# Attention and quantised FFN on one core: the FFN rows transposed by a DMA in place of TensorE and ScalarE

## The chip, the core and the metric

One NeuronCore of a Trainium2 chip. The metric is the time of one execution on the device in microseconds, the median of several runs. The engines are TensorE (PE, its weight loads PEld), VectorE (DVE), ScalarE (ACT), GpSimd (POOL) and SyncE (SP, which issues the DMAs).

## What is computed

x and ctx have the shape (128, 64, 128): 8192 tokens of 128 features. The reference, cut to what matters:

```
x = x + attention(layernorm(x), ctx, ctx)        # 16 heads of 64, causal, softmax
x = x + ffn(layernorm(x))

def bitlinear(x, w):                             # rows of x are quantised to 8 bits, w to -1, 0, 1
    scale = 127.0 / clip(max(abs(x), axis=-1), 1e-05)
    return einsum('bsi,oi->bso', round(x * scale) / scale, ternary(w))
ffn(x) = bitlinear(silu(bitlinear(x, w_gate)) * bitlinear(x, w_up), w_down)   # inner width 512
```

The change concerns the input of the last bitlinear: 128 tokens x 512 quantised numbers, held as whole numbers in bf16 (`hid_b`). The matmul with w_down needs them with the 512 features on partitions (`hid_t`, four blocks of 128x128).

## The kernel before

The tokens are cut into 64 pairs (two sequences of 64 tokens, 128 rows each), and 16 groups of four pairs. One slot of every engine's program handles one pair in each stage at once; the stages are staggered. In slot s (numbered from 0):

- pair s: scores (TensorE L425), bias and row maximum (VectorE L738, L741), subtraction (GpSimd L866), exponential (ScalarE L570), row sum (VectorE), scaling (GpSimd L884);
- pair s-1: transposes of the probabilities in two halves (TensorE L453 to ps_a, then ps_b), copies to prob_t on ScalarE, attention output (L494), residual x1 (VectorE L801), second layernorm and quantisation, xq;
- pair s-2: transpose of xq (TensorE L438), copy to xq_t (ScalarE), gate and up matmuls (L466, L467), tanh (ScalarE L606), gated, hid, hid_q (VectorE L754, L768, L785), and hid_b (GpSimd L876, signals hb_ready);
- pair s-3: transposes of hid_b (TensorE L446, into the bank ps_b), copy to hid_t (ScalarE, signals ht_evac), down matmul (TensorE L482, signals down_ready), x2 (VectorE L763).

Between these TensorE computes quarters of the next group's keys (k_quarter, L316 to L318, three matmuls of 512 columns each, copied by ScalarE to kp) and of this pair's values (v_quarter, L396 to L398, copied to vp). The last group has no next group, so its slots (60 to 63) have no key quarters. Slots 64 to 66 drain the stages. Every engine takes its program strictly in order; semaphores are the only synchronisation. The transposes of hid_b stand in slots 3 to 66, that is in 64 slots.

The order on TensorE in a slot is: scores, transpose of xq, transposes of hid_b, first half of the probabilities, gate and up (after xq_t), v_quarter 0, second half, k_quarter 0, down matmul, v and k quarters 1, attention output, v and k quarters 2, k_quarter 3, v_quarter 3. In the first slot of a group v_quarter 0 comes ahead of the transpose of xq. After the last slot of a group four transposes of ctx and four of x follow. On ScalarE the order is: xq_t, hid_t, first half of prob_t, tanh, vp and prob_t in turn, kp, vp, exponential, kp, vp, kp, kp, vp.

SP's queue holds all loads and stores. Per group it issues x and ctx of the group after next, x again for the residual (x_res), and the store of the group before.

Of the kernel before, what the change touches and what calls it, by code (L numbers as in the profile page):

```python
# [32 lines left out]
P = 128  # L33
# [7 lines left out]
def build(nc, x, ctx, mask, wq, wk, wv, wo, bo, w_gate, w_up, w_down, ident, causal, chooser, out):  # L41
# [19 lines left out]
    with ExitStack() as es:  # L61
# [9 lines left out]
        ps_h = ps_b[:, 0:F // 2].bitcast(BF16)  # L71
# [53 lines left out]
        id_bf = sb("id_bf", [P, P], BF16)  # L125
# [40 lines left out]
        pt_ready, attn_ready, xqt_ready, gate_ready, up_ready, ht_ready, down_ready = (sem(n) for n in (  # L166
            "pt_ready", "attn_ready", "xqt_ready", "gate_ready", "up_ready", "ht_ready", "down_ready"))

        ctxt_evac, xnt_evac, k_evac, v_evac, pt_evac, xqt_evac, ht_evac, exp_done, tanh_done = (sem(n) for n in (
            "ctxt_evac", "xnt_evac", "k_evac", "v_evac", "pt_evac", "xqt_evac", "ht_evac", "exp_done", "tanh_done"))  # L170
# [38 lines left out]
        def _(sp):  # L209
# [19 lines left out]
            def group(it, par):  # L229

                g = 2 * it + par
                dyn = lambda v, k: v[g + k] if isinstance(it, int) else v[bass.ds(g + k, 1)].rearrange(
                    "o p q d -> (o p) q d")
                if group_ahead(it, par * GP, 2):
                    sp.wait_ge(xn_ready, GP * g + GP)
                    sp.dma_start(x_in[par][:], dyn(x_g, 2)).then_inc(x_loaded[par], 16)
                    sp.wait_ge(ctxt_ready, g + 1)
                    sp.dma_start(ctx_in[par][:], dyn(ctx_g, 2)).then_inc(ctx_loaded[par], 16)
                if group_ahead(it, par * GP, 1):
                    if not isinstance(it, int) or g:  # L240
                        sp.wait_ge(x1_done, GP * g)
                    sp.dma_start(x_res[1 - par][:], dyn(x_g, 1)).then_inc(xres_loaded[1 - par], 16)
                if not isinstance(it, int) or g:
                    sp.wait_ge(x2_done, GP * g)
                    sp.dma_start(dyn(out_g, -1), x1[1 - par][:]).then_inc(stored[1 - par], 16)

            for it in range(BODIES):
                for par in range(2):
                    group(it, par)
# [10 lines left out]
        def _(pe):  # L260
# [116 lines left out]
            def slot(it, c):  # L377
# [64 lines left out]
                if live(it, c, 3):  # L442

                    pe.wait_ge(hb_ready, s - 2)
                    for k in range(FB):
                        t = nc.tensor.transpose(ps_h[:, k * P:(k + 1) * P], hid_b[:, k * P:(k + 1) * P], id_bf[:])  # L446
# [468 lines left out]
```

## Time and profile before

| | |
|---|---|
| median of 3 runs | 815.12 us (815.04 to 815.55) |
| the profiled execution | 815.8 us, span 814.0 us |
| busy: TensorE, VectorE, ScalarE, GpSimd | 783.2, 677.9, 678.6, 406.9 us |
| granted TensorE clock over the span | 0.993 of full speed |
| DMA packets' share of the 16 DMA engines, SP's queue | 8.5% |
| setup: cast of id_bf on VectorE at 4.99 us | 0.21 us, and then 0.56 us of waiting for a mask matmul (L268) |

The busy time of an engine includes overlap of pipelined instructions, so a busy TensorE is not one at its peak. The idle time of an engine that is not the bottleneck costs nothing. A row of the timeline says when an instruction (or several alike, "x4") starts, for how long it is recorded, and in brackets how long its engine stood idle ahead of it and for whom.

### The profile page before, as it was taken

The page shows a single profiled execution, that of the slowest core. Times are in us where ns is not written, and L with a number is a line of the kernel's source. Part 1 is how long each engine was busy: PE and PEld are TensorE (multiplying, and loading weights), DVE is VectorE, ACT ScalarE, POOL GpSimd, SP SyncE. Part 2 cuts the span into 40 slices and gives each one's busy share as a digit, 9 for nine tenths or more (in the row PEclk, how much of TensorE's full clock was granted, in tenths as well). Part 3 has the DMA queues.
Part 4 walks back from the last instruction along what each step waited for, and adds up shares of the span by engine and source line. Part 5 has one row for each costly group of instructions (what it writes and reads, how often), then busy time and mean ns, then how long its engine had stood idle before and what let it go on. Part 6 is the DMA issues. An engine that isn't in the chain of part 4 may idle for free.

```text
span 814.0 us, 15482 instructions
## 1 busy us (share of the span) xinstructions
PE 783.2 (96%) x5487; PEld 543.7 (67%) x5550; DVE 677.9 (83%) x1845; ACT 678.6 (83%) x1202; POOL 406.9 (50%) x404
## 2 busy tenths in 40 slices
PE   7899999999999999999999999999999999999983
PEld 5657667666766766666676676676676667667652
DVE  7749888888888888888888888888888888878894
ACT  4688888888888888988888888888888888888872
POOL 1234545455455555555555545555455554544551
PEclk9999999999999999999999999999999999999997
DMA  7200010000101001010100101010010100000000
GB/s 219 61 1 1 15 39 16 22 18 14 41 13 40 5 17 33 14 41 14 39 1 14 41 14 40 14 40 2 13 41 14 40 14 15 0 14 14 2 14 14
DMA packets 37123, 20.84 MB, mean 26 GB/s; under 512 B 1460, under 2 KB 36534, under 8 KB 37046
## 3 DMA queue, kind: packets, MB, share of 16 engines
q1 hardware_dynamic: 37046, 19.84, 8.5%
q8 instruction: 45, 0.74, 0.4%
q14 instruction: 32, 0.26, 0.1%
HBM read 15.64 MB, written 4.19 MB: 24 GB/s over the span
## 4 chain that ended last, share of the span: by engine, by line
PE 91%; DVE 4%; ACT 2%; issue 2%; POOL 1%; DMA 0%; POOLq 0%; DVEq 0%
PE ps_s L425 14%; PE ps_a L494 14%; PE ps_s L396 5%; PE ps_s L316 4%; PE ps_kv L396 4%; PE ps_kv L397 3%; PE ps_kv L316 3%; PE ps_kv L317 3%; PE ps_s L318 3%; PE ps_s L398 3%; PE ps_s L397 3%; PE ps_b L453 3%; PE ps_s L317 3%; PE ps_kv L398 3%; PE ps_kv L318 3%; PE ps_a L453 3%
## 5 line engine op out<-in xcount | busy, mean ns | idle before, releaser
L866 POOL TENSOR_TENSOR prob<-prob,row_max 128x1024 f32<-128x1024 f32 x64 | 121.9, 1905 | 179.6 <-DVE row_max L741 179.6
L514 ACT ACTIVATE vp<-ps_s 64x512 f32<-64x512 f32 x256 | 151.2, 591 | 33.2 <-PE ps_s L398 28.9
L884 POOL TENSOR_TENSOR prob<-prob,row_rec 128x512 f32<-128x512 f32 x128 | 130.7, 1042 | 56.5 <-DVE row_rec L816 56.5
L514 ACT ACTIVATE vp<-ps_kv 64x512 f32<-64x512 f32 x256 | 151.5, 592 | 5.3
L876 POOL TENSOR_TENSOR hid_b<-hid_q,neg_round 128x512 bf16<-128x512 f32 x64 | 66.5, 1039 | 124.3 <-DVE hid_q L785 124.3
L494 PE MATMUL ps_a<-vp,prob_t 128*64 128x128 f32 x2048 | 125.9, 276 | 1.3 <-DVE x L763 1.2
L494 PEld LDWEIGHTS ps_a<-vp,prob_t 128*64 128x64 f32 x2048 | 110.6, 137 | 24.3 <-issue 16.3
L425 PE MATMUL ps_s<-kp,xn_t 128*64 128x512 f32 x512 | 124.0, 605 | 2.9 <-ACT vp L514 1.9
L738 DVE TENSOR_TENSOR prob<-ps_s,bias_sb 128x1024 f32<-128x1024 f32 x64 | 78.4, 1225 | 51.8 <-PE ps_s L425 51.7
L843 POOL TENSOR_TENSOR rs<-ve,neg_half 128x1 f32<-128x1 f32 x128 | 70.2, 548 | 42.0 <-DVE ve L663 25.0
L514 ACT ACTIVATE kp<-ps_s 128x512 f32<-128x512 f32 x130 | 77.8, 598 | 11.8 <-PE ps_s L284 8.0
L741 DVE TENSOR_REDUCE row_max<-prob 128x16 f32<-128x1024 f32 x64 | 78.1, 1220 | 2.2
L814 DVE TENSOR_REDUCE row_sum<-prob 128x16 f32<-128x1024 f32 x64 | 77.4, 1210 | 0.0
L514 ACT ACTIVATE kp<-ps_kv 128x512 f32<-128x512 f32 x122 | 72.3, 593 | 0.6 <-PE ps_kv L284 0.5
L425 PEld LDWEIGHTS ps_s<-kp,xn_t 128*64 128x64 f32 x512 | 31.0, 136 | 60.4 <-issue 55.3
L514 ACT ACTIVATE xq_t<-ps_u 128x128 bf16<-128x128 f32 x64 | 17.8, 278 | 62.7 <-PE ps_u L438 62.7
L570 ACT ACTIVATE prob<-prob 128x1024 f32<-128x1024 f32 x64 | 66.9, 1045 | 0.0
L396 PE MATMUL ps_s<-n_hi,ct_hi 128*128 128x512 f32 x128 | 62.5, 489 | 0.7 <-ACT vp L514 0.7
L396 PE MATMUL ps_kv<-n_hi,ct_hi 128*128 128x512 f32 x128 | 61.4, 480 | 0.0
L316 PE MATMUL ps_kv<-ct_hi,m_hi 128*128 128x512 f32 x120 | 52.5, 438 | 1.0 <-ACT wd_t L514 1.0
L754 DVE SCALAR_TENSOR_TENSOR gated<-tanh_sb,ps_g 128x512 f32<-128x512 f32 x64 | 43.9, 687 | 10.2 <-ACT tanh_sb L606 8.8
L316 PE MATMUL ps_s<-ct_hi,m_hi 128*128 128x512 f32 x128 | 52.0, 406 | 0.3
(175 smaller groups left out, 1734.8 us busy)
## 6 DMA issues: line engine op xcount, KB each, us to landing
x_in<-in_x SPq DMA_DIRECT2D x16, 256.0 KB, 3.9
ctx_in<-in_ctx SPq DMA_DIRECT2D x16, 256.0 KB, 4.4
x_res<-in_x SPq DMA_DIRECT2D x16, 256.0 KB, 2.8
out<-x SPq DMA_DIRECT2D x15, 256.0 KB, 2.5
kp<-in_L_xattn_Wk SPq DMA_DIRECT2D x1, 512.0 KB, 3.7
kp<-in_L_xattn_Wq SPq DMA_DIRECT2D x1, 512.0 KB, 4.6
kp<-in_L_xattn_Wv SPq DMA_DIRECT2D x1, 512.0 KB, 5.5
kp<-in_L_xattn_Wo SPq DMA_DIRECT2D x1, 512.0 KB, 6.1
```

The costliest lines, as they stand in the source:

```text
L316: mm(dst, hi, ct_hi[par][:], start=True, stop=False)
L396: mm(v_dst, ct_hi[par][:, cols], hi, start=True, stop=False)
L425: t = mm(ps_s[b * S:(b + 1) * S, half * BANK:(half + 1) * BANK], xn_t[par][:, cols], kp[par][:, half * 8:half * 8 + 8, cols], start=True, ...
L494: t = mm(ps_a[b * S:(b + 1) * S, 0:D], prob_t[:, a, b * S:(b + 1) * S], vp[(c - 1) % 2][:, b, a, :], start=(a == 0), stop=(a == HP - 1))
L514: copy = lambda dst, src, **kw: nc.scalar.activation(dst, src, ACT.Copy, **kw)
L570: nc.scalar.activation(prob[c % 2][:], prob[c % 2][:], ACT.Exp).then_inc(exp_done, 1)
L738: v.tensor_tensor(prob[c % 2][:], ps_s[:, :].rearrange("p (h j) -> p h j", j=S), pair_bias.broadcast_to([P, H, S]), ALU.add).then_inc(bias ...
L741: v.tensor_reduce(row_max[c % 2][:], prob[c % 2][:], AX, ALU.max).then_inc(max_done, 1)
L814: v.tensor_reduce(row_sum[:], prob[c % 2][:], AX, ALU.add).then_inc(sum_step, 1)
L843: p.tensor_tensor(dst[:], src[:], neg_half[:], ALU.pow).then_inc(done, 1)
L866: p.tensor_tensor(prob[c % 2][:], prob[c % 2][:], rows(row_max[c % 2]), ALU.subtract).then_inc(shifted, 1)
L884: p.tensor_tensor(prob[c % 2][:, heads, :], prob[c % 2][:, heads, :], rows(row_rec[c % 2])[:, heads, :], ALU.mult).then_inc(normed, 1)
```

## The change

The four transposes of hid_b on TensorE and the copy to hid_t on ScalarE go away, and with them the bf16 identity id_bf and its cast in the setup. SP issues one transposing DMA from SBUF to SBUF per pair: once hid_b is written and the previous down matmul has read hid_t. The down matmul waits for that DMA (ht_moved), as does GpSimd's next write of hid_b. SP's loads and stores are laid out slot by slot around it: the store of the group before in the last slot of a group ahead of the transpose, x_res in its second slot and x and ctx in its third slot behind the transpose. The waits of loads and stores on the compute engines are the same; x and ctx are now asked for by the group three ahead.

```
@@ SP
-            def group(it, par):
-                ... x_in and ctx_in of group g+2, x_res of group g+1, store of group g-1
+            def load_inputs(g):
+                par = g % 2
+                sp.wait_ge(xn_ready, GP * (g - 2) + GP)
+                sp.dma_start(x_in[par][:], x_g[g]).then_inc(x_loaded[par], 16)
+                sp.wait_ge(ctxt_ready, g - 1)
+                sp.dma_start(ctx_in[par][:], ctx_g[g]).then_inc(ctx_loaded[par], 16)
+            def slot(it, c):
+                s = BODY * it + c
+                g, q, par = 2 * it + c // GP, c % GP, c // GP % 2
+                if q == 3 and g > 0 and live(it, c):
+                    sp.wait_ge(x2_done, GP * g)
+                    sp.dma_start(out_g[g - 1], x1[1 - par][:]).then_inc(stored[1 - par], 16)
+                if live(it, c, 3):
+                    sp.wait_ge(hb_ready, s - 2)
+                    if live(it, c, 4):
+                        sp.wait_ge(down_ready, s - 3)
+                    sp.dma_start_transpose(hid_t[:, :, :], hid_b[:, :]).then_inc(ht_moved, 16)
+                if q == 1 and live(it, c) and group_ahead(it, c, 1):
+                    if g:
                         sp.wait_ge(x1_done, GP * g)
+                    sp.dma_start(x_res[1 - par][:], x_g[g + 1]).then_inc(xres_loaded[1 - par], 16)
+                if q == 2 and live(it, c) and group_ahead(it, c, 3):
+                    load_inputs(g + 3)
+            load_inputs(2)
+            slots(slot, 3)
@@ TensorE
-                if live(it, c, 3):
-                    pe.wait_ge(hb_ready, s - 2)
-                    for k in range(FB):
-                        t = nc.tensor.transpose(ps_h[:, k * P:(k + 1) * P], hid_b[:, k * P:(k + 1) * P], id_bf[:])
-                    t.then_inc(ht_ready, 1)
@@ TensorE, second half of the probabilities
-                    if live(it, c, 3):
-                        pe.wait_ge(ht_evac, s - 2)
@@ TensorE, down matmul
-                    pe.wait_ge(ht_evac, s - 2)
+                    pe.wait_ge(ht_moved, 16 * (s - 2))
@@ ScalarE
-                if live(it, c, 3):
-                    act.wait_ge(ht_ready, s - 2)
-                    copy(flat(hid_t[:, :, :]), ps_h[:, :]).then_inc(ht_evac, 1)
@@ VectorE, setup
-            dve.wait_ge(id_in, 16)
-            v.tensor_copy(id_bf[:], id_sb[:]).then_inc(const_set, 1)
@@ GpSimd, before hid_b
-                        pool.wait_ge(ht_ready, s - 2)
+                        pool.wait_ge(ht_moved, 16 * (s - 2))
```

## Rows read from the trace of the kernel before

**Rows 1.** Busy time of each engine in a stretch: engine busy (count), clock, DMA.

```profile
105.40:405.40 300.00, 298.54 (x2104) 206.46 (x2128) 257.07 (x710) 260.50 (x464) 158.74 (x157) 1.00 0.09 25
...
746.00:795.00 49.00, 43.42 (x344) 29.75 (x346) 43.43 (x117) 40.38 (x72) 28.27 (x26) 1.00 0.02 7
...
795.00:814.00 19.00, 6.38 (x60) 4.26 (x59) 9.50 (x30) 3.57 (x7) 2.62 (x3) 0.69 0.05 15
```

**Rows 2.** The same view for hid_b alone, steady stretch.

```profile
105.40:405.40 300.00, 9.66 (x100) 8.73 (x100) 25.97 (x25) 1.00 0.09 25
```

**Rows 3.** Timeline of a plain slot: start, duration, engine, line, operation, idle before.

```profile
407.38 0.39 PE L446 MATMUL ps_b<-id_bf,hid_b 128*128 128x128 bf16 x4
...
407.58 0.28 ACT L514 ACTIVATE xq_t<-ps_u 128x128 bf16<-128x128 f32 x1 [0.69 <-PE ps_u L438]
...
407.60 0.61 PE L453 MATMUL ps_a<-id_sb,prob 128*128 128x128 f32 x4
...
407.94 0.10 PEld L466 LDWEIGHTS ps_g<-wg_t,xq_t 128*128 128x128 bf16 x1
```

**Rows 4.** Timeline of the same slot: hid_b, down matmul, next hid_b.

```profile
402.38 1.04 POOL L876 TENSOR_TENSOR hid_b<-hid_q,neg_round 128x512 bf16<-128x512 f32 x1 [1.74 <-DVE hid_q L785]
...
410.32 0.40 PE L482 MATMUL ps_a<-wd_t,hid_t 128*128 128x128 bf16 x4
...
414.04 1.04 POOL L876 TENSOR_TENSOR hid_b<-hid_q,neg_round 128x512 bf16<-128x512 f32 x1 [1.74 <-DVE hid_q L785]
```

**Rows 5.** Timeline of slot 65: xq_t and the gate's weight load.

```profile
803.21 0.28 ACT L514 ACTIVATE xq_t<-ps_u 128x128 bf16<-128x128 f32 x1 [6.75 <-PE ps_u L438]
...
803.54 0.10 PEld L466 LDWEIGHTS ps_g<-wg_t,xq_t 128*128 128x128 bf16 x1 [0.21 <-ACT xq_t L514]
```

**Rows 6.** Waits from 100 to 700 us: total, times, longest.

```profile
PEld ps_s L316 <- ACT kp L514: 5.5, 12, 0.5
```

**Rows 7.** Timeline of the first slot of a group, parts.

```profile
420.89 0.61 PE L453 MATMUL ps_a<-id_sb,prob 128*128 128x128 f32 x4
...
421.09 0.60 ACT L514 ACTIVATE hid_t<-ps_b 128x512 bf16<-128x512 bf16 x1
...
421.58 0.59 ACT L514 ACTIVATE prob_t<-ps_a 128x512 f32<-128x512 f32 x1
...
427.01 0.40 PE L397 MATMUL ps_s<-n_lo,ct_hi 128*128 128x512 f32 x1
...
427.24 0.39 PE L398 MATMUL ps_s<-n_hi,ct_lo 128*128 128x512 f32 x1
...
427.66 0.19 PEld L316 LDWEIGHTS ps_s<-ct_hi,m_hi 128*128 128x128 f32 x1 [0.46 <-ACT kp L514]
```

**Rows 8.** Timeline of slot 64, VectorE.

```profile
796.00 0.69 DVE L754 SCALAR_TENSOR_TENSOR gated<-tanh_sb,ps_g 128x512 f32<-128x512 f32 x1 [2.22 <-ACT tanh_sb L606]
```

**Rows 9.** DMA issues: KB each, us from issue to landing.

```profile
ctx_in<-in_ctx SPq DMA_DIRECT2D x16, 256.0 KB, 4.4
...
id_sb<-c_ident SPq DMA_DIRECT2D x1, 64.0 KB, 1.8
```

**Rows 10.** Timeline of the last slots: hid_b, down matmul, its use.

```profile
780.20 1.04 POOL L876 TENSOR_TENSOR hid_b<-hid_q,neg_round 128x512 bf16<-128x512 f32 x1 [1.49 <-DVE hid_q L785]
...
786.32 0.39 PE L482 MATMUL ps_a<-wd_t,hid_t 128*128 128x128 bf16 x4
...
799.56 1.04 POOL L876 TENSOR_TENSOR hid_b<-hid_q,neg_round 128x512 bf16<-128x512 f32 x1 [5.05 <-DVE hid_q L785]
...
804.37 0.63 PE L482 MATMUL ps_a<-wd_t,hid_t 128*128 128x128 bf16 x4
...
805.51 0.34 DVE L763 SCALAR_TENSOR_TENSOR x<-ps_a,o_scale,x 128x128 f32<-128x128 f32 x1
...
808.47 1.04 POOL L876 TENSOR_TENSOR hid_b<-hid_q,neg_round 128x512 bf16<-128x512 f32 x1 [7.31 <-DVE hid_q L785]
...
810.86 0.61 PE L482 MATMUL ps_a<-wd_t,hid_t 128*128 128x128 bf16 x4 [0.69 <-ACT hid_t L514]
```

More of the change, by code:

```diff
@@ L70, in build @@
         ps_b = ps("ps_b", 1)
-        ps_h = ps_b[:, 0:F // 2].bitcast(BF16)
         ps_g = ps("ps_g", 1)
@@ L124, in build @@
         hid_b = sb("hid_b", [P, F], BF16)
-        id_bf = sb("id_bf", [P, P], BF16)
         hid_t = sb("hid_t", [P, FB, P], BF16)
@@ L165, in build @@
             "ctxt_ready", "xnt_ready", "k_ready", "v_ready", "scores_ready"))
[L166 to L170, printed above, removed]
+        pt_ready, attn_ready, xqt_ready, gate_ready, up_ready, ht_moved, down_ready = (sem(n) for n in (
+            "pt_ready", "attn_ready", "xqt_ready", "gate_ready", "up_ready", "ht_moved", "down_ready"))
+        ctxt_evac, xnt_evac, k_evac, v_evac, pt_evac, xqt_evac, exp_done, tanh_done = (sem(n) for n in (
+            "ctxt_evac", "xnt_evac", "k_evac", "v_evac", "pt_evac", "xqt_evac", "exp_done", "tanh_done"))
         ctlo_ready, biased, max_done, sum_step, ln1_step, xn_ready = (sem(n) for n in (
@@ L227, in _ @@
             sp.dma_start(x_res[0][:], x_g[0]).then_inc(xres_loaded[0], 16)
-            def group(it, par):
[L231 to L240, printed above, removed]
-                        sp.wait_ge(x1_done, GP * g)
[L242 to L245, printed above, removed]
@@ L247, in _ @@
-            for it in range(BODIES):
-                for par in range(2):
-                    group(it, par)
+            def load_inputs(g):
[17 more added lines that the diff above has]
+                    if g:
+                        sp.wait_ge(x1_done, GP * g)
+                    sp.dma_start(x_res[1 - par][:], x_g[g + 1]).then_inc(xres_loaded[1 - par], 16)
+                if q == 2 and live(it, c) and group_ahead(it, c, 3):
+                    load_inputs(g + 3)
@@ L334, in _ @@
                     pe.wait_ge(absum_done, 3)
-                    pe.wait_ge(const_set, 4)
+                    pe.wait_ge(const_set, 3)
                     mm(ps_kv[:, 0:3], ones_sb[:], f_sum[:, 0:3], start=True, stop=True).then_inc(mean_ready, 1)
```

## The prediction

> **What bounds the kernel now.** I read the busy time by stretch first. In the steady part TensorE is busy 298.54 of 300 us; in the 49 us of the last group (no next group to prepare) it is busy 43.42 and VectorE 43.43; in the last 19 us TensorE has 6.38 us of work, so the tail is latency [rows 1]. One slot handles one pair, and 25 slots fit in 300 us, 12.0 us each on average [rows 2]. So the question in 58 of the 64 affected slots (3 to 60) is how much earlier TensorE reaches its next instruction, and not how busy ScalarE is.
>
> Next I read the timeline around the removed instructions [rows 3]. In a plain slot (third or fourth pair of a group, some 11.66 us from one hid_b to the next [rows 4]) TensorE transposes xq (released xq_t), then hid_b (407.38), then the first half of the probabilities (407.60), then loads the weights of the gate matmul (407.94). That load needs xq_t, which ScalarE finishes at 407.58 + 0.28 = 407.86. The reader should see that the removed transposes stand between a request and its answer: xq goes out to ScalarE, and TensorE does 0.22 + 0.34 us of other work until the answer is back.
>
> **What is removed from TensorE.** Four transposes of hid_b per slot (100 in 25 slots [rows 2]), which overlap each other; what they add to the queue is the distance from their start to the next instruction's, 407.60 - 407.38 = 0.22 us [rows 3]. Taken off in full that is 58 x 0.22 = 12.8 us. It does not come off in full: without them the probability transposes start at 407.38 and the gate's weight load could start 0.22 earlier, at 407.72, but xq_t is finished only at 407.86. Of the wake-up, the tail has a row in which TensorE really waits: xq_t ends at 803.21 + 0.28 = 803.49, the load starts at 803.54, 0.05 later [rows 5]. So the load moves from 407.94 to 407.91. The gain is 0.03 us per slot, 58 x 0.03 = 1.7 us; the other 0.19 turns from work into waiting for xq_t. ScalarE has been idle for 0.69 us when xq arrives [rows 3], so it can't answer sooner when its hid_t copy is gone.
>
> **What is removed from ScalarE.** One copy of 0.60 us per slot [rows 7]. It pays only where ScalarE makes TensorE wait. That is once per group: in its first slot the load of L316 waits 0.5 us for a kp copy, 12 times in the 600 us [rows 6]. There ScalarE runs from xq_t to that kp copy without a gap. The copy of the first half of the probabilities starts at 421.58, behind hid_t; without it, it starts as soon as its transposes end, 420.89 + 0.61 - 0.22 = 421.28, so about 0.3 earlier, which two queued neighbours leave at 0.27. TensorE's matmuls here follow each other at 0.23 us (L397 at 427.01, L398 at 427.24); L316 starts 0.42 us after L398 (427.24 to 427.66), so 0.19 us is lost to ScalarE, and 0.27 covers it [rows 7]. 14 such slots (4, 8, ... 56) x 0.19 = 2.7 us. In slot 64 VectorE waits 2.22 us for tanh [rows 8], which stands behind the same pair of copies: 0.3 us. In slots 61 to 63 VectorE starts its work back to back; I cost them at nothing, hidden by VectorE's 43.43 us; without that cover it would be 0.03 each.
>
> **What is added: the transpose by DMA.** Call T the time from hid_b's last write to the moment TensorE may load hid_t: SP's wake-up, issue, transfer, completion. No row of before shows such a transfer. From below: 64 KB plain takes 1.8 us from issue to landing; from above among plain ones: 256 KB behind another 256 KB takes 4.4 us [rows 9]. This one moves 128 KB inside the chip; I take the middle of these, T = 3.0. A reordering transfer may be slower than any plain one, so what hides it matters more:
> - Plain slots: hid_b ends at 402.38 + 1.04 = 403.42, the down matmul (L482) starts at 410.32: 6.90 us of cover, and all of T disappears behind TensorE's own matmuls.
> - Slots 61 to 64: 781.24 to 786.32, 5.08 us of cover.
> - Slot 65: 800.60 to 804.37, 3.77 us, and VectorE takes the result (L763) only at 805.51, 0.51 after the matmul ends at 805.00; so it costs from about T = 4.2.
> - Slot 66: nothing covers it. Hid_b ends at 809.51 and the matmul starts at 810.86, 1.35 us for transposes, copy and hand-overs; in place of them stands T. Cost T - 1.35 = 1.65 us.
> All of these are read in [rows 4, 10].
>
> The new wait of SP is on hb_ready and on the previous down matmul, which ends at 410.72 where the next hid_b ends at 415.08, so hb_ready is always last [rows 4]. Behind it in SP's queue stand loads and stores. The x_res load and the loads three groups ahead are issued right behind a transpose, some 8 us before or about where they were issued, and have slots of 12 us to land; the store of a group is issued before that slot's transpose as its x2 is complete earlier. Only in the drain does something queue: the store of three quarters of the last group, ready at about 805.9, now waits until the transpose of slot 66 is issued near 809.6; it hides behind the very last store, which can't be issued before x2 of the last pair, near 812. GpSimd's new wait (transfer before the next hid_b) has a whole slot, 11.66 - T. VectorE loses one small cast in the setup, after which it waited for TensorE (the table of the profile above): nothing.
>
> The page "VectorE: DVE Perf Modes" of the Trainium skill, section "The three transpose paths", speaks against the change: 390 ns on TensorE against 1309 ns by the DMA crossbar for a 128x128 bf16 block, and its rules for authors prefer TensorE where PSUM will do. Here TensorE pays 0.22 us for four blocks in its queue [rows 3], so for TensorE the trace is lower than the page; for the crossbar no row here can tell. Four times 1309 is an estimate of 5.2 us by that page; by it the sum below would come out at about no change.
>
> **Sum, T = 3.0:** -1.7 (TensorE queue) - 2.7 (first slots of groups) - 0.3 (slot 64) + 1.65 (slot 66) = -3.05 us. The profiled execution took 815.8 us with a span of 814.0; the median of the runs is 815.12, and I take the difference to it: 812.1 us.
>
> **Rivals.**
> - Full queue gain. If the wait for xq_t is shorter than I read, all 0.22 us come off in 58 slots: 11.1 us more gain, 801.0. For it: TensorE is the bound at 99.5% in the steady part. Against: 407.86 and 407.94 above [rows 3]. 0.07.
> - Transfer of middle length, T from 4.4 to 5.3: the steady part still hides it, but slot 66 costs 3.1 to 4.0, slot 65 0.2 to 1.1 and slots 61 to 64 up to 1.0 together. Sum from -1.5 to +1.4: no change, 813.6 to 816.5. The sum of the skill's estimate falls here. 0.20.
> - Longer, T from 5.3 to 6.9: the last group pays in four slots. At 6.7: -4.7 + 5.35 + 2.5 + 4 x 1.65 = +9.8, 825. 0.07.
> - The transfer becomes the bound (the slower side): its place is the loop down matmul, x2, hid, hid_q, hid_b, transpose, next down matmul. From L482 at 410.32 to the end of the next hid_b (414.04 + 1.04 = 415.08) are 4.76 us [rows 4, 10], so a slot can't be shorter than 4.76 + T, and against the mean of 12.0 [rows 2] this decides from T of about 7.0 to 7.2. Four blocks one after another, each at the 1.8 us of the 64 KB row [rows 9], would give T = 7.2: then the gains are gone, and the end costs 5.85 + 3.0 + 4 x 2.1 = 17: 832 us. Each further microsecond of T adds some 57 us. For it: a transfer that writes 2-byte elements in another order has no plain row as its equal. Against: 6.9 us is much for 128 KB. 0.14.
>
> **Chances and range.** My forecast (T up to 4.4, small queue gain) 0.52, its own range 810.5 to 814. With the 0.07 of the full gain: faster 0.59. Within 0.2% (1.6 us, about what can be told): the middle length, 0.20. Slower: 0.07 + 0.14 = 0.21. The range 808 to 826 holds the forecast, the middle and the longer case and, below, a queue gain of up to twice what I expect; it leaves out the full gain and the transfer as bound, together 0.21.
>
> **What would show it.** (1) Transposes gone from TensorE, and in their place an idle of about 0.2 us before the gate matmul's weight load, released by xq_t: right. No such idle and slots 0.2 us shorter: full gain. (2) The 0.5 us wait of L316 for kp gone in first slots of groups. (3) Landing of the transpose against the start of L482: over 3 us of room in plain slots; a wait of L482 for DMA there would make me wrong. (4) From the last hid_b to the last L482 about 3.0 us instead of 1.35. (5) The prediction fails most cheaply by T: above 4.4 the gain is gone, above 7 it turns into a large loss.

## The result, and the profile after

| | before | after |
|---|---|---|
| median of 4 runs | 815.34 us (815.04 to 816.84) | 807.38 us (807.29 to 807.77) |
| ratio to before | | 0.990, 95% interval 0.9883 to 0.9915 |
| span of the profiled execution | 814.0 us | 805.3 us |
| busy: TensorE, ScalarE | 783.2, 678.6 us | 776.1, 653.8 us |

The change makes the kernel 8.0 us faster. Later runs beside other kernels gave 806.42 us (806.2 to 806.91) for the same code, ratio 0.9887 (0.9874 to 0.9901). The forecast was faster, by 3.05 us.

From the page of the changed kernel: span, busy time, DMA packets, SP's queue, and the issues of the new transfer (the last number is the median time from issue to landing).

```profile
span 805.3 us, 15033 instructions
...
PE 776.1 (96%) x5294; PEld 527.6 (66%) x5294; DVE 678.5 (84%) x1844; ACT 653.8 (81%) x1138; POOL 407.0 (51%) x404
...
DMA packets 71937, 29.19 MB, mean 36 GB/s; under 512 B 36277, under 2 KB 71351, under 8 KB 71863
...
q1 hardware_dynamic: 71862, 28.24, 13.7%
...
hid_t<-hid_b SPq DMA_TRANSPOSE x64, 2.5
```

The unknown of the prediction, the transfer's time, is in the last line: 2.5 us. SP's queue goes from 8.5% to 13.7% of the DMA engines' time. The busy time says nothing on the gain: TensorE still counts as busy all the time in the steady stretch, which answers to the first row of [rows 1]:

```profile
105.40:405.40 300.00, 300.00 (x2052) 202.79 (x2049) 261.03 (x714) 254.23 (x445) 160.57 (x159) 1.00 0.14 36
```

TensorE's recorded instructions overlap, so a hole of a tenth of a microsecond doesn't show in this sum, and the gain has to be read from distances between starts. I take the start of the gate matmul's weight load (L466 in both kernels) as the mark of a slot.

| stretch | before | after | difference |
|---|---|---|---|
| up to the first mark (slot 2) | 61.20 | 60.26 | -0.94 |
| slot 2 to 3 | 11.26 | 11.22 | -0.04 |
| slots 3 to 59, 56 steps | 670.96 | 661.62 | -9.34 |
| slots 59 to 63 | 41.22 | 40.96 | -0.26 |
| 63 to 64, 64 to 65 | 9.80, 9.10 | 9.82, 9.46 | +0.38 |
| slot 65's mark to the end of the last hid_b | 5.97 | 5.96 | -0.01 |
| end of the last hid_b to the last down matmul | 1.35 | 2.54 | +1.19 |

The sum is -9.02 us; the store behind the last work takes 0.3 us more, and the spans differ by 8.7 us. Inside the 56 steps the median step from a group's first slot to its second goes from 11.32 to 11.05 us (-0.27, 14 times), the other three steps of a group by 0.13 each (11.66 to 11.53, 11.67 to 11.53, 13.29 to 13.16; 42 times): 14 x 0.27 + 42 x 0.13 = 9.2 us. This trace is on the long side: a second trace of the same code (e15) has 11.51 us for the plain slots and 660.78 us for the 56 steps, 10.2 us less than before.

The plain slot of the changed kernel, which answers to [rows 3, 4]: start, duration, engine, line, operation, in brackets the idle time and its releaser.

```profile
401.71 0.33 PE L444 MATMUL ps_u<-id_sb,xq 128*128 128x128 f32 x1
...
401.88 0.60 PE L453 MATMUL ps_a<-id_sb,prob 128*128 128x128 f32 x4
...
402.08 0.28 ACT L512 ACTIVATE xq_t<-ps_u 128x128 bf16<-128x128 f32 x1 [0.69 <-PE ps_u L444]
...
402.41 0.10 PEld L466 LDWEIGHTS ps_g<-wg_t,xq_t 128*128 128x128 bf16 x1 [0.17 <-ACT xq_t L512]
...
402.41 0.39 PE L466 MATMUL ps_g<-wg_t,xq_t 128*128 128x512 bf16 x1
...
402.64 0.38 PE L467 MATMUL ps_u<-wu_t,xq_t 128*128 128x512 bf16 x1
...
404.69 0.40 PE L480 MATMUL ps_a<-wd_t,hid_t 128*128 128x128 bf16 x4
```

The reader is to see two things. The weight load now waits 0.17 us for xq_t, and it and its matmul start at the same time, 402.41. And from the transpose of xq (401.71) to the up matmul (402.64) are 0.93 us. In the kernel before, where that transpose starts at 407.21, it is 1.05 us to 408.26; three rows of its timeline:

```profile
407.21 0.33 PE L438 MATMUL ps_u<-id_sb,xq 128*128 128x128 f32 x1
...
408.05 0.10 PEld L467 LDWEIGHTS ps_u<-wu_t,xq_t 128*128 128x128 bf16 x1
...
408.26 0.38 PE L467 MATMUL ps_u<-wu_t,xq_t 128*128 128x512 bf16 x1
```

The two matmuls follow each other at some 0.22 us, so before the change the gate matmul started at about 408.04 (its own record is missing), 0.10 us after its weights had been loaded at 407.94. The load was ahead of its matmul then; it set nothing.

The waits of the changed kernel from 100 to 700 us (total, times, longest), which answer to [rows 6]:

```profile
PEld ps_g L466 <- ACT xq_t L512: 8.5, 51, 0.2
...
PEld ps_s L322 <- ACT kp L512: 4.8, 12, 0.4
```

The wait for xq_t is in all 51 slots of the stretch, 0.17 us each. The wait for the kp copy in the first slots of groups is still there, 0.1 us shorter.

The end of the kernel, timeline, which answers to the last rows of [rows 10]:

```profile
798.26 1.04 POOL L869 TENSOR_TENSOR hid_b<-hid_q,neg_round 128x512 bf16<-128x512 f32 x1 [7.15 <-DVE hid_q L778]
...
799.33 1.19 SPq L246 DMA_TRANSPOSE hid_t<-hid_b  x1
...
801.84 0.61 PE L480 MATMUL ps_a<-wd_t,hid_t 128*128 128x128 bf16 x4 [7.04 <-DMA hid_t<-hid_b]
```

Nothing covers the transfer here, so T can be read off: from 798.26 + 1.04 = 799.30 to 801.84, 2.54 us: 0.03 until SP issues, 2.45 for the DMA, 0.05 until TensorE starts. The page "VectorE: DVE Perf Modes" of the Trainium skill, section "The three transpose paths", gives 1309 ns for one 128x128 block; four of them would be an estimate of 5.2 us. The trace gives half of that for the four blocks moved by one instruction, and the trace decides.

### The profile page after: what moved, and what is told of

It reads as the page before. It is cut to its first block, busy times and chain, and to the rows that moved or that the text cites. A ratio compares the mean times of both kernels' runs of the same rounds, so it can differ in the third digit from the quotient of the medians.

```text
span 805.3 us, 15033 instructions
## 1 busy us (share of the span) xinstructions
PE 776.1 (96%) x5294; PEld 527.6 (66%) x5294; DVE 678.5 (84%) x1844; ACT 653.8 (81%) x1138; POOL 407.0 (51%) x404
## 2 busy tenths in 40 slices
DMA packets 71937, 29.19 MB, mean 36 GB/s; under 512 B 36277, under 2 KB 71351, under 8 KB 71863
## 3 DMA queue, kind: packets, MB, share of 16 engines
q1 hardware_dynamic: 71862, 28.24, 13.7%
## 4 chain that ended last, share of the span: by engine, by line
PE 89%; DVE 7%; issue 1%; DMA 1%; ACT 1%; POOL 1%; POOLq 0%; DVEq 0%
PE ps_s L431 14%; PE ps_a L492 14%; PE ps_s L402 5%; PE ps_s L322 4%; PE ps_kv L402 4%; PE ps_kv L322 4%; PE ps_s L403 3%; PE ps_s L324 3%; PE ps_s L404 3%; PE ps_kv L323 3%; PE ps_s L323 3%; PE ps_kv L403 3%; PE ps_kv L324 3%; PE ps_kv L404 3%; PE ps_a L453 3%; PE ps_b L453 3%
## 5 line engine op out<-in xcount | busy, mean ns | idle before, releaser
L512 ACT ACTIVATE kp<-ps_s 128x512 f32<-128x512 f32 x130 | 77.7, 598 | 11.9 <-PE ps_s L290 8.1
L322 PE MATMUL ps_kv<-ct_hi,m_hi 128*128 128x512 f32 x120 | 52.6, 438 | 1.0 <-ACT wd_t L512 1.0
L322 PE MATMUL ps_s<-ct_hi,m_hi 128*128 128x512 f32 x128 | 52.0, 406 | 0.0
L403 PE MATMUL ps_s<-n_lo,ct_hi 128*128 128x512 f32 x128 | 50.7, 396 | 0.0
```

The lines of the kernel that those rows point to most:

```text
L322: mm(dst, hi, ct_hi[par][:], start=True, stop=False)
L403: mm(v_dst, ct_hi[par][:, cols], lo, start=False, stop=False)
L512: copy = lambda dst, src, **kw: nc.scalar.activation(dst, src, ACT.Copy, **kw)
```

## The experiments

Each kernel was timed against the kernel before on the same chip; ratios are to it. "Plain slot" is the median of the second and third of a group's four steps, "first slot" the step from the first slot of a group to its second. After: 11.53 (e15: 11.51) and 11.05 us; before: 11.66 and 11.32 us.

### e1: the setup's cast put back

```
+            dve.wait_ge(id_in, 16)
+            v.tensor_copy(id_bf[:], id_sb[:]).then_inc(const_set, 1)
...
-                    pe.wait_ge(const_set, 3)
+                    pe.wait_ge(const_set, 4)
```

> The changed kernel with only the setup's cast of id_bf, its wait for the identity and TensorE's count of four put back; nothing uses id_bf. Theory (the 0.9 us that the setup is shorter comes from the moment at which TensorE's matmuls go from double to single duration, not from the cast): 807.4 us give or take 0.9, and the transposes of the setup change their duration from about 1.06 us for four to 0.60 at one place or the other. Rival (the cast and its wait delayed the setup): 808.3 us, with VectorE's work after the cast later by 0.2 us or more.

Measured: 807.58 us (806.59 to 808.43), ratio 0.9894 (0.9879 to 0.9908). The slots are those of the changed kernel (first slot 11.04, 56 steps 661.34). The first mark is at 61.08, near the 61.20 of before; but the changed kernel run again, without the cast, had it at 61.22. So the cast is not what the 0.94 us of the setup came from. What differs is read from TensorE's timeline in the setup. Before:

```profile
12.11 1.06 PE L274 MATMUL ps_g<-id_sb,ctx_in 128*128 128x128 f32 x4
...
12.96 1.06 PE L284 MATMUL ps_a<-id_sb,kp 128*128 128x128 f32 x4
...
13.81 0.65 PE L284 MATMUL ps_b<-id_sb,kp 128*128 128x128 f32 x4
```

After:

```profile
11.90 0.60 PE L280 MATMUL ps_g<-id_sb,ctx_in 128*128 128x128 f32 x4
...
12.34 0.60 PE L290 MATMUL ps_a<-id_sb,kp 128*128 128x128 f32 x4
...
12.78 0.60 PE L290 MATMUL ps_b<-id_sb,kp 128*128 128x128 f32 x4
```

The same four transposes take 1.06 us in one trace and 0.60 in the other, and the moment of the change differs by over a microsecond. The changed kernel run again (e15) has the 1.06 us of the kernel before at this place. Over the seventeen traces the first mark lies anywhere from 60.26 to 62.35. What moves it was not settled; it belongs to no edit that was tried.

### e2 and e3: four or two transposes of hid_b back on TensorE, with the DMA kept

The results of these transposes are not used; ScalarE copies nothing and hid_t still comes by DMA. GpSimd waits for them before it writes the next hid_b. The bf16 identity and its cast, which e1 tested, come back with them.

```
+                if live(it, c, 3):
+                    pe.wait_ge(hb_ready, s - 2)
+                    for k in range(4):          # e3: range(2)
+                        t = nc.tensor.transpose(ps_h[:, k * P:(k + 1) * P], hid_b[:, k * P:(k + 1) * P], id_bf[:])
+                    t.then_inc(ht_ready, 1)
```

> The changed kernel with the four transposes of hid_b put back on TensorE at their old place, their result unused; hid_t still comes by DMA and ScalarE has no copy. Theory (0.13 us per slot came off TensorE's queue in 58 slots, and 0.14 us more in 14 first slots of groups came from ScalarE): 7.5 us come back, about 814.9 us, slots of 11.66 us and first-slot to second-slot distances of 11.18 us. Rival (the queue term was 0.03 per slot as predicted and ScalarE's copy gave the rest): 809.1 us.

> The same with two of the four transposes put back (0.11 us of queue in place of 0.22). Theory (the gate matmul starts at the later of two moments: the end of the matmuls queued ahead of it, and the arrival of xq_t): two transposes end 0.02 us after xq_t's arrival, so only 0.02 us per slot, 1.2 us in all: 808.6 us. Rival (what is taken off the queue pays in proportion): half of 7.5 us, 811.1 us.

Measured: e2 816.91 us (816.16 to 819.23), ratio 1.0014 (1.0004 to 1.0023); e3 809.99 us (809.37 to 810.19), ratio 0.9924 (0.9908 to 0.9941). Over the 56 steps e2 takes 670.57 us, against 670.96 before and 661.62 after: 8.95 of the 9.34 us come back with the four transposes alone. Plain slots take 11.66 in e2, but 11.54 to 11.56 in e3: the first two transposes cost about 0.02 us (0.03 to 0.05 against e15) and the next two 0.11. So the 0.22 us that four of them occupy is not what is saved; the gate matmul starts at the later of two moments, the end of the queue ahead of it or the arrival of xq_t. First slots take 11.28 in e2 and 11.17 in e3, so there each pair costs about 0.12.

The timeline of e2 has the record that is missing in the kernel before:

```profile
407.75 0.61 PE L462 MATMUL ps_a<-id_sb,prob 128*128 128x128 f32 x4
...
408.09 0.10 PEld L475 LDWEIGHTS ps_g<-wg_t,xq_t 128*128 128x128 bf16 x1
...
408.20 0.38 PE L475 MATMUL ps_g<-wg_t,xq_t 128*128 128x512 bf16 x1
...
408.41 0.38 PE L476 MATMUL ps_u<-wu_t,xq_t 128*128 128x512 bf16 x1
```

With the four transposes in the queue the gate's load (408.09) runs 0.11 us ahead of its matmul (408.20), which starts 0.45 us, four transposes at 0.11, after 407.75. Without them both start together. This is the point at which the prediction went wrong.

### e4: ScalarE's copy back, with the DMA kept

```
+                if live(it, c, 3):
+                    act.wait_ge(hb_ready, s - 2)
+                    copy(hid_x[:], hid_b[:, :]).then_inc(ht_evac, 1)
```

The copy reads hid_b itself and its result is not used; GpSimd waits for it as well.

> The changed kernel with ScalarE's copy of 128x512 bf16 put back at its old place, reading hid_b in SBUF and writing a spare tile (the old one read PSUM); TensorE has no transposes. Theory: the first slots of groups lose what they had gained, 14 x 0.14 us, and the other slots nothing: 809.3 us. Rival (the copy was what held up most slots): 814.9 us.

Measured: 810.71 us (810.62 to 810.89), ratio 0.9933 (0.9918 to 0.9947). Plain slots stay at 11.51, first slots go to 11.30, 0.25 above the changed kernel. The wait for the kp copy grows (waits from 100 to 700 us):

```profile
PEld ps_s L323 <- ACT kp L513: 7.9, 12, 0.7
```

So the copy costs nothing in plain slots and a quarter of a microsecond once per group, 14 x 0.25 = 3.5 us; the time rose by 3.3. With e2, either half of the removed work is enough to lose nearly all of the 0.27 us there: TensorE's 0.22 us alone (e2) or ScalarE's 0.60 us copy alone (e4). A first slot that is as long as the slower of two paths, TensorE's and ScalarE's, and gets shorter only if both do, fits all four lengths: 11.32 with both (before), 11.28, 11.30, and 11.05 with neither.

### e5: more work ahead of the gate matmul

If TensorE idles 0.09 us for xq_t, independent work ahead of the gate matmul should fill it. Here that is the whole v_quarter 0 (three matmuls), and in the first slots the second half of the probabilities.

```
+                if early:
+                    second_half()
+                    gate_up()
+                elif group_ahead(it, c, 1):
+                    v_quarter(0)
+                    gate_up()
+                    second_half()
```

> The changed kernel with other work between the transpose of xq and the gate matmul: v_quarter 0 ahead of gate and up in plain slots, the second half of the probabilities' transposes ahead of them in first slots. Theory (what is left of the removed transposes' 0.22 us, 0.09 us per slot, is waiting for xq_t): 58 x 0.09 = 5.2 us less, 802.2 us, and no wait of the gate's weight load for xq_t. Rival (tanh comes 0.7 us later and VectorE, which has 0.85 us to spare before it needs it, is held up together with what follows): 807 to 810 us.

Measured: 810.04 us (809.13 to 810.86), ratio 0.9931 (0.9916 to 0.9946). Over the 56 steps it takes 662.64 us, against 660.78 and 661.62 in two traces of the changed kernel. The wait for xq_t is gone and the one for the kp copy, which was in first slots only, is now in every slot (waits from 100 to 700 us):

```profile
PEld ps_s L322 <- ACT kp L525: 17.8, 51, 0.7
```

In a plain slot the up matmul now starts 1.54 us after the transpose of xq, 0.61 later than in the changed kernel, and ScalarE's tanh 1.74 us after it, 0.44 later; behind tanh stand the kp copies. TensorE waits 0.25 us for one of them, and the plain slot is 11.49 us, so of the 0.09 about 0.02 is gained. The loss is in the first slots, where the second half of the probabilities was moved. Here the edit shifts the mark itself, so I take VectorE's row maximum instead: from a group's first slot to its second it is 11.97 us, against 11.79 in e15, 14 times. My theory that the order would bring the gain was wrong for this size of move: ScalarE became what TensorE waits for. The rest of the distance to 807.38 lies at the two ends of the kernel, and the section on the prediction shows how much these scatter.

### e6: the last pair by TensorE and ScalarE

```
-                if live(it, c, 3):
+                if live(it, c, 3) and not (s - 3 >= PAIRS - 1):
                     ... dma_start_transpose
+                if live(it, c, 3) and s - 3 >= PAIRS - 1:
+                    ... four transposes on TensorE, and the copy on ScalarE, as before
```

> The changed kernel, but the very last pair's hid_b (slot 66) is transposed by TensorE and copied by ScalarE as before the change. Theory (the drain lost 2.54 - 1.35 = 1.2 us to the transfer): 806.2 us. Rival (the end is set by the stores, so the transfer hides): 807.4 us.

Measured: 804.67 us (804.44 to 805.87), ratio 0.9868 (0.9854 to 0.9883). The end of its timeline:

```profile
798.45 1.04 POOL L891 TENSOR_TENSOR hid_b<-hid_q,neg_round 128x512 bf16<-128x512 f32 x1 [7.30 <-DVE hid_q L797]
...
799.54 0.61 PE L455 MATMUL ps_b<-id_bf,hid_b 128*128 128x128 bf16 x4 [4.56 <-POOL hid_b L891]
...
800.19 0.60 ACT L524 ACTIVATE hid_t<-ps_b 128x512 bf16<-128x512 bf16 x1 [5.33 <-PE ps_b L455]
...
800.84 0.61 PE L492 MATMUL ps_a<-wd_t,hid_t 128*128 128x128 bf16 x4 [0.69 <-ACT hid_t L524]
```

From hid_b's end to the down matmul are 1.35 us again, in place of 2.54. That is the loss of the drain, 1.2 us, taken back where nothing covers the transfer. The whole time fell by more, 2.7 us against the first runs of the changed kernel and 1.75 against e15; the two other pairs with this edit give 1.9 (e10 to e11) and 1.1 (e13 to e14). Of these only the 1.2 is seen at its place.

### e7, e8, e9: one, three and five further transposes ahead of the real one

They go to buffers that nobody reads, and make T longer.

```
+                    for i in range(n):
+                        sp.dma_start_transpose(hid_x[i][:, :, :], hid_b[:, :]).then_inc(extra_moved, 16)
                     sp.dma_start_transpose(hid_t[:, :, :], hid_b[:, :]).then_inc(ht_moved, 16)
```

> The changed kernel with one more transposing DMA of hid_b, into a spare tile, issued ahead of each real one. Theory (a transfer is hidden as long as it lands within the cover): landing comes later by one issue, 1.2 us, to about 3.7 us; the steady part does not change, slot 66 pays 1.2: 808.6 us. Rival (the transfers' traffic itself slows the engines or the loads): 57 slots longer by a visible amount, 812 us or more.

> Three more transposing DMAs ahead of each real one. Theory: landing at about 2.5 + 3 x 1.2 = 6.1 us; the plain slots' cover of about 6.6 us still hides it; slots 61 to 63 (cover about 5.1) lose 1.0 each, slot 64 and 65 about 3, slot 66 3.6: 816 to 818 us, with slots of 11.53 us as before. Rival (traffic or SP's queue hold up the steady part): 825 us or more.

> Five more transposing DMAs ahead of each real one. With three the gap from hid_b to the last down matmul was 6.47 us against 2.54 without, 1.31 per transfer, so T is about 9.1 us here. Theory (loop: down matmul, x2, hid, hid_b, transfers, next down matmul; a slot can't be shorter than 4.76 + T = 13.9 us): 57 slots of about 13.9 in place of a mean of 11.8, and the last ones in place of 9.7, some 945 us. Rival (only what exceeds the cover of 6.6 us is paid, once per slot, and the following slots recover part of it): 870 us or less.

Measured: e7 808.55 us (806.62 to 809.23), ratio 0.9909 (0.9891 to 0.9927), slots as in the changed kernel (56 steps 660.66) and 3.85 us in the last gap. e8 826.97 us (825.95 to 828.79), ratio 1.0141 (1.0125 to 1.0157), last gap 6.47 us. e9, a single run, 968.23 us. The end of e7's timeline shows what each further transpose adds:

```profile
799.29 1.19 SPq L250 DMA_TRANSPOSE hid_x<-hid_b  x1
...
800.52 1.27 SPq L251 DMA_TRANSPOSE hid_t<-hid_b  x1
...
803.12 0.60 PE L486 MATMUL ps_a<-wd_t,hid_t 128*128 128x128 bf16 x4 [7.97 <-DMA hid_t<-hid_b]
```

SP takes 1.2 to 1.3 us to issue one, and the next is issued behind it; from its own issue each lands in 2.6. So T grows by the issue, 1.3 us, and not by the 2.5 us of a transfer. In e7 T is 3.85 and all of it is hidden but in the drain, and twice as many transposes slow down nothing else in the steady part. In the drain slot 65 pays too, 1.5 us: the transpose issued at 790.10 took 4.39 us to land, and the down matmul waited for it until 794.54.

In e8 T is 6.47 where it can be read, and the cover of a plain slot of the changed kernel is about 6.65 us (hid_b's end, one slot before 408.54 + 1.04, to L480 at 404.69). The median slot is indeed still 11.51, but the 56 steps take 669.46 us, 8 more. Its waits from 100 to 700 us:

```profile
PEld ps_a L486 <- DMA hid_t<-hid_b: 14.6, 26, 1.6
```

This count is to be read with care. The same load stands idle for 0.27 us in plain slots of the changed kernel, which wait for no DMA (its waits in the same stretch):

```profile
PEld ps_a L480 <- issue: 13.5, 50, 0.3
```

Of the 26 waits of e8, 15 are this 0.27. The other 11 are real, 0.35 to 1.6 us, and in ten of them the transpose of hid_t took 3.2 to 4.2 us from its issue to its landing, where 2.55 is usual. Over all of e8, 28 of 256 transposes took over 2.7 us, up to 4.8. Such late landings are there without e8's queue as well, only rarer: 3 of 128 in e7 (up to 4.4), 1 of 64 in the changed kernel (3.26), none in e15. What makes one late was not settled. I had counted with the median landing and missed by some 10 us, 8 of them here. In e9 every slot waits (its timeline):

```profile
406.89 7.16 SPq L250 DMA_TRANSPOSE hid_x<-hid_b  x5
...
414.10 1.27 SPq L251 DMA_TRANSPOSE hid_t<-hid_b  x1
...
416.70 0.40 PE L486 MATMUL ps_a<-wd_t,hid_t 128*128 128x128 bf16 x4 [2.79 <-DMA hid_t<-hid_b]
```

From 406.87, hid_b's end, to 416.70 T is 9.8 us, and a slot is 416.70 - 402.22 = 14.5: the loop that the prediction's fourth rival describes, 4.76 + 9.8 = 14.6. This is one of the longer slots, in which SP took 7.16 us to issue the five; most often it takes 6.4 to 6.5 us, T is 9.1 and a step from one hid_b to the next 13.75 us, against 4.76 + 9.1 = 13.9. Longer slots and late landings bring the mean to 14.1, which is about half of the 23 us that the expectation of 945 missed. The rival's mechanism is real; the change is far from it.

### e10, e11, e12: the transpose of xq between the halves of the scores

This asks for xq_t earlier, so that it is back before the queue ends: in the changed kernel (e10), there with the last pair by TensorE (e11), and in the kernel before (e12), slots 4 to 59.

```
                     for half in range(2):
+                        if half == 1 and mid_scores:
+                            transpose_xq()
                         for b in range(2):
                             ... scores
```

> The changed kernel with TensorE's transpose of xq moved ahead, between the two halves of the scores, in slots 4 to 59. Theory (TensorE waits 0.09 us per slot for xq_t since the four transposes are gone, and nothing else is bound there as long as the gate isn't delayed): plain slots of 11.43 us in place of 11.53, about 5 us less than the changed kernel, ratio to the kernel before about 0.984. Rival (ScalarE is the next bound right behind, as in the run with v_quarter 0 ahead of the gate): plain slots stay within 0.03 of 11.5.

> The same, and the last pair's hid_b transposed by TensorE and copied by ScalarE. Theory: another 1.2 us less, ratio about 0.982, the fastest version here. Rival: as for the run before it, then 0.987.

> The kernel before, with nothing but the transpose of xq moved ahead as in the two runs above. Theory (before the change the four transposes filled the time until xq_t came, so TensorE did not wait for it): ratio 1.000 give or take 0.001, plain slots 11.66. Rival (the move pays by itself, whatever the transposes do): 0.994 or lower.

Measured: e10 822.87 us (821.25 to 824.39), ratio 1.0088 (1.007 to 1.0106); e11 820.93 us (820.12 to 821.14), ratio 1.0061 (1.0044 to 1.0078); e12 832.88 us (831.22 to 833.05), ratio 1.0207 (1.0191 to 1.0222). All are slower; neither theory had that. The timeline of e10:

```profile
407.53 2.04 POOL L882 TENSOR_TENSOR prob<-prob,row_rec 128x512 f32<-128x512 f32 x2 [0.87 <-DVE row_rec L814]
...
407.67 1.08 PE L440 MATMUL ps_s<-kp,xn_t 128*64 128x512 f32 x4
...
408.36 0.29 DVE L828 TENSOR_SCALAR xq<-xn,qs 128x128 f32<-128x128 f32 x1
...
408.80 0.30 PE L392 MATMUL ps_u<-id_sb,xq 128*128 128x128 f32 x1
...
410.04 0.66 PE L458 MATMUL ps_a<-id_sb,prob 128*128 128x128 f32 x4
```

From the first half of the scores to the transposes of the probabilities are now 410.04 - 407.67 = 2.37 us, against 2.03 in the changed kernel. The place was too early: VectorE ends xq only at 408.36 + 0.29 = 408.65, and its transpose starts 0.15 us behind that, at 408.80. That 0.15 is the median of all 50 slots of the stretch from 100 to 700 us; in the changed kernel the transpose starts 1.0 us after xq's end. The four scores ahead of it, at the 0.23 us of the changed kernel, would have let it start at 408.60, so 0.20 of the 0.34 us is TensorE waiting for xq. The other 0.14 (a slower resumption of the scores) is not explained. GpSimd is not what held up the probability transposes: it ended at 407.53 + 2.04 = 409.57, 0.47 us before them. Plain slots take 11.81 us in e10 and 11.9 to 12.0 in e12, some 0.3 more than without the move in both kernels. So a request can't be asked before its own input is there. The pair e12 and e10 still says one thing, with the move in both: the mean distance between two hid_b is 12.27 and 12.08 us, so the change is worth 0.20 us per slot there, against 11.98 - 11.81 = 0.17 without the move. That is consistent with an answer that comes early bringing a little more of the 0.22, and not all; two traces are little to show it.

### e13 and e14: one matmul ahead of the gate

The size of the hole is 0.09 us, the smallest piece of other work 0.22 us in the queue: the first of v_quarter 0's three matmuls, and in first slots one transpose of the second half. The rest stays where it was. e14 has e6's last pair as well.

```
+                split = s >= 4 and not early and live(it, c) and group_ahead(it, c, 1)
+                if split:
+                    v_quarter(0, 1)                  # its first matmul
                 ... gate and up
-                    v_quarter(0)
+                    v_quarter(0, 2 if split else 0)  # the other two
```

> The changed kernel with one instruction group between the first half of the probabilities and the gate matmul: one of the three matmuls of v_quarter 0 in plain slots, one of the four transposes of the second half in first slots; from slot 4 on. Theory (the 0.09 us wait for xq_t is all that is left, and a gate later by 0.14 us does not delay tanh, which stands behind a copy on ScalarE): plain slots 11.44 us in place of 11.53, no wait of the gate's load for xq_t, first slots unchanged as ScalarE sets them: 43 x 0.09 = 3.9 us less than the changed kernel. Rival (ScalarE binds TensorE in every slot): no change.

> The same, and the last pair's hid_b transposed by TensorE and copied by ScalarE. Theory: 3.9 + 1.2 us less than the changed kernel, ratio to before about 0.984. Rival: 1.2 us less, 0.988.

> The changed kernel itself once more, beside the two others. Both theories: ratio to before 0.990, give or take 0.001; what differs from the first profile is only when TensorE's durations change in the setup and in the last slots, 1 us at either end.

Measured on one chip: e13 803.69 us (803.06 to 803.81), ratio 0.9851 (0.9838 to 0.9865); e14 802.57 us (801.63 to 803.51), ratio 0.9842 (0.9828 to 0.9855); the changed kernel again (e15) 806.42 us, ratio 0.9887 (0.9874 to 0.9901). Plain slots fall to 11.44 us, the 56 steps to 658.19 (e15 660.78). The gain is 2.7 us, where 3.9 was expected: it is 0.07 us in the plain slots and nothing in the first ones. The timeline of e13 in a plain slot, and its wait for xq_t from 100 to 700 us:

```profile
400.44 0.33 PE L450 MATMUL ps_u<-id_sb,xq 128*128 128x128 f32 x1
...
401.27 0.10 PEld L479 LDWEIGHTS ps_g<-wg_t,xq_t 128*128 128x128 bf16 x1 [0.15 <-ACT xq_t L525]
...
401.51 0.38 PE L480 MATMUL ps_u<-wu_t,xq_t 128*128 128x512 bf16 x1
```

```profile
PEld ps_g L479 <- ACT xq_t L525: 4.1, 27, 0.2
```

From the transpose of xq to the up matmul are 1.07 us, of which 0.22 is a matmul moved here from later: 0.85 against 0.93, 0.08 less, what the hole held. The load still shows a wait of 0.15 us in its row and waits in 27 slots, where the expectation had no wait; from one up matmul to the next the slot is shorter all the same: a waiting weight load is not yet a waiting TensorE. Tanh, the next of ScalarE's work, starts 1.29 us after the transpose of xq, 1.30 in the changed kernel. The wait for the kp copy, which e5 had spread to every slot, stays at 12 times here. e14 beats both kernels, by 1.6% the one before and, 802.57 to 806.42, by 3.9 us the changed one.

## Why the prediction was wrong in size

The direction, the bound (TensorE in the steady part), and the cover of the transfer in all but the last slot were right. The sum was -3.05 us against -8.0. In the table the 0.03 us that the forecast gave to the queue in every slot stands in the first slots' row where it concerns them.

| term | forecast | measured | which runs show it |
|---|---|---|---|
| TensorE's queue, 44 slots | 44 x -0.03: -1.3 | 42 x -0.13 and -0.26 from slot 59 to 63: -5.7 | after, e2, e3 |
| first slots of groups | 14 x (-0.03 - 0.19): -3.1 | 14 x -0.27: -3.8 | after, e2, e4 |
| slot 64 | -0.3 | -0.4 and -0.2 where the clock is full | e15, e7, e4; below |
| drain | +1.65 | +1.19 | after, e6, e7 |
| store at the end | 0 | +0.3 | not tested |
| setup | 0 | -0.94 | no edit; scatter |

**The step that failed** is "So the load moves from 407.94 to 407.91. The gain is 0.03 us per slot". It took the start of the gate's weight load for the pace of TensorE, and so mis-sized the queue's gain per slot, 0.03 us for 0.13. That load was already 0.10 us ahead of its own matmul, behind four transposes still running, so 407.94 was not what the removal moves. The matmul's start was: 407.60 + 4 x 0.11 = 408.04 before. After, in the same times, it is the later of 408.04 - 0.22 = 407.82 (queue) and 407.86 + 0.05 = 407.91 (xq_t, with load and matmul together), so 407.91: 0.13 us per slot. This is what the median slots show (0.13), and e3 and e2 put it back in the two unequal steps that the rule of the later moment gives (0.02, then 0.11). The page "TensorE: Matmul & The Clock Gate" of the Trainium skill, section "Architectural detail: the array is 16× 32×32, not 1× 128×128", says that TensorE's queue can pull a weight load ahead of matmuls in flight; e2's rows 408.09 and 408.20 agree. This is also where "every engine takes its program strictly in order", in the description of the kernel, is too strong: it holds for the matmuls here, and a weight load starts ahead of earlier matmuls' end.

**First slots.** The prediction gave 0.19, what ScalarE cost TensorE there, beside the queue's 0.03, and the step shrank by 0.27, as much as it had worked out for ScalarE's whole shift. I had treated the two removals as independent, capping one at the idle time it caused. TensorE's own work ahead also became shorter, so TensorE could follow ScalarE all the way. The sign of this is that the wait of L322 for the kp copy did not go (5.5 to 4.8 us, 12 times), although point (2) of what I would look for had said so. That each removal alone gives almost nothing (e2: 11.28, e4: 11.30, before 11.32, both: 11.05) was not expected.

**The wait for xq_t**, point (1): 0.17 us in place of an idle of about 0.2. Right; but of it only 0.09 is time that TensorE loses, and e13, which fills it, gains 0.07.

**The transfer**, T = 2.54 against 3.0: 0.46 less loss in the drain. The bounds 1.8 and 4.4 held it. The store queued in the drain, which the prediction had hidden, may have a part in the 0.3 us that the end takes longer behind the last down matmul; no run tells it apart. Points (3) and (4) are right in kind: in the plain slots 6.65 - 2.54, some 4 us of room, and one exposed transfer. e6 takes the loss back, e7 shows the room, e8 and e9 where it ends.

**Slot 64 and the setup.** From slot 64's mark to slot 65's the distance is 9.10 before and 9.46 after, and over the further kernels but e9 from 8.72 to 10.64 us, with nothing changed there in most. It goes with TensorE's granted clock just behind slot 64's mark, as the five microseconds from there show (busy time of each engine, then the clock, DMA share and GB/s): first the kernel before, then the changed one in its two traces (after, e15), then e1.

```profile
794.40:799.40 5.00, 3.43 (x44) 2.65 (x43) 3.23 (x9) 2.05 (x4) 0.12 (x1) 1.00 0.02 3
```

```profile
783.90:788.90 5.00, 4.38 (x44) 3.43 (x42) 2.90 (x7) 1.77 (x3) 0.00 (x0) 0.74 0.00 0
```

```profile
783.80:788.80 5.00, 3.11 (x42) 2.63 (x42) 3.48 (x9) 1.66 (x3) 0.21 (x2) 1.00 0.00 0
```

```profile
784.30:789.30 5.00, 4.33 (x35) 3.83 (x36) 3.31 (x8) 1.77 (x3) 0.21 (x2) 0.56 0.00 0
```

In these slots TensorE has no key quarters and idles, 2.64 us ahead of the transpose of xq at 783.02 in after and 2.79 us ahead of the same one at 793.74 in before. Why the clock falls at one moment or another is not settled. Taking only traces at 1.00 settles the prediction's -0.3 for slot 64 fairly well: 9.10 before, 8.72 in e15 and 8.86 in e7, both without ScalarE's copy, and 9.09 in e4, which has the copy back. So some 0.2 to 0.4 us came off, and e4 points to the copy. The +0.36 of the profiled pair goes with the lower clock.

About 2 us at the setup and as much at the end can differ between two traces of this family. The 0.94 us of the setup in the profiled pair is of that kind. The terms that the change did cause (-5.7, -3.8, -0.3 for slot 64, +1.2, +0.3) add up to -8.3, near the 8.0 and 9.0 us by which the two sets of runs differ from the kernel before.

**The rivals.** Full queue gain (0.22 in every slot, 801.0): no, 0.13. A transfer of 4.4 or more: no, 2.54. The loop as the bound: no at T = 2.54; yes at 9.8 (e9). The time lies between the forecast and the first rival, because the true answer to "all or nothing of 0.22" was 0.13.

## What to carry to other kernels

When work is removed from an engine's queue ahead of a wait, compute the start of the next matmul (not of its weight load, which runs ahead) as the later of queue end and arrival, before and after; the difference is the gain, and what is left is a hole whose size tells how much other work may be moved into it. Fill such a hole with a piece of its own size: one matmul gained 2.7 us here (0.07 us per plain slot), three matmuls 0.02 us per plain slot, since they delayed the next engine. A transfer off the critical path costs nothing while its latest landing, not its median, fits the cover; in a drain nothing covers it, and here the old path was 1.2 us shorter there. When two traces are compared at their ends, take stretches that begin at the same instruction, and set distances side by side only at the same granted clock.

## What the runs showed of the hardware that was not expected

- A transposing DMA of 128x512 bf16 from SBUF to SBUF lands 2.5 us after its issue (median of 64, 2.4 to 3.3), although it moves its 128 KB in many small packets: the 64 of them added some 34,800 (71937 in all, 37123 before), nearly all under 512 B. The plain 64 KB load of the identity takes 1.8 before and 1.9 after. The transpose's issue holds SP for 1.19 us, 1.27 when another stands before it, and a row of them is spaced by that and not by the transfer (e7 to e9).
- Some landings are late: 3 of 128 in e7 (up to 4.4 us), 28 of 256 in e8 (up to 4.8). In e8 they, not the median, set what the steady part lost.
- A weight load behind running matmuls starts 0.10 to 0.11 us ahead of its matmul; when it had to wait for its data, both are recorded at the same start (402.41), and the load adds nothing visible.
- In the setup the same four 128x128 f32 transposes take 1.06 or 0.60 us, from a moment that differs by 1 us between kernels, while the granted clock is given as 1.00 in both traces (10 to 14 us). Near the end of the changed kernel four transposes of this form take 1.06 us again (at 784.94), and there the granted clock from 784 to 786 us is 0.50.
